# First normalization of a two-layer graph network moved into the second layer's block, with that layer's first builds

## What is computed

```python
def _L0_gnn_ref(node_feat, edge_feat, eps, src, dst):
    m = jax.nn.relu(node_feat[src] + edge_feat)
    neigh = jax.ops.segment_sum(m, dst, num_segments=node_feat.shape[0])
    return (1.0 + eps[0]) * node_feat + neigh

def _L1_gnn_ref(node_f, src, dst):
    n = node_f.shape[0]
    ones = jnp.ones(src.shape[0], dtype=node_f.dtype)
    out_deg = jnp.clip(jax.ops.segment_sum(ones, src, num_segments=n), 1.0)
    in_deg = jnp.clip(jax.ops.segment_sum(ones, dst, num_segments=n), 1.0)
    x = node_f * jax.lax.rsqrt(out_deg)[:, None]
    agg = jax.ops.segment_sum(x[src], dst, num_segments=n)
    return agg * jax.lax.rsqrt(in_deg)[:, None]

x = _layernorm(x + _L0_gnn_ref(x, edge_attr_32, L0_gnn_eps, src, dst), axis=-1)
x = _layernorm(x + _L1_gnn_ref(x, src, dst), axis=-1)
```

## Time and profile before

| | us |
|---|---|
| median of 3 runs | 5204.33 (5204.24 to 5209.14) |
| the profiled execution | 5206.82, its span 5205.0 |
| `layer_0`, first instruction to the last on DVE | 0 to 3949.0 |
| `finish_0`, first PE instruction to the last on DVE | 3951.0 to 3987.2 |
| `layer_1`, first on DVE to the last addition into `acc` | 3988.1 to 5167.6 |
| `finish_1`, from its first transpose | 5170.1 on |

### The profile page before, as it was taken

How to read it: one execution, slowest core, us unless ns; L and a number is a source line. 1 busy time by engine, 2 the same in 40 slices (tenths; PEclk the granted TensorE clock), 3 DMA queues, 4 the chain that set the end, 5 groups by cost and what they waited for, 6 DMA issues and landing times. The chain is left out here.

```text
span 5205.0 us, 62766 instructions
## 1 busy us (share of the span) xinstructions
PE 3317.5 (64%) x21148; PEld 1678.5 (32%) x21148; DVE 3284.0 (63%) x4730; ACT 2758.7 (53%) x2908; POOL 2961.1 (57%) x3134
## 2 busy tenths in 40 slices
PE   4555555555555555555555555555555999999997
PEld 1111111111111111111111111111113888888886
DVE  7766666666666666666666666666665444444445
ACT  4555555555555555555555555555554555555553
POOL 7777777777777777777777777777771000000000
PEclk7666666666666666666666666666666999999998
DMA  3333333333333333333333333333334999999995
GB/s 126 119 122 133 125 119 119 120 125 136 125 119 119 119 119 139 122 119 119 121 127 133 125 119 119 119 122 136 123 116 160 325 323 325 324 324 325 324 326 206
DMA packets 269134, 867.71 MB, mean 167 GB/s; under 512 B 90218, under 2 KB 140218, under 8 KB 252602
## 3 DMA queue, kind: packets, MB, share of 16 engines
q1 hardware_dynamic: 169107, 815.98, 42.2%
q0 software_dynamic: 100000, 51.40, 6.1%
HBM read 486.77 MB, written 380.38 MB: 167 GB/s over the span
## 5 line engine op out<-in xcount | busy, mean ns | idle before, releaser
L163 POOL DMA_INDIRECT rows<-in_x,src_t x3125 | 2959.4, 947 | 961.7 <-issue 947.2
L687 PE MATMUL built<-x_parts,b_hot 100*128 100x490 bf16 x3000 | 1291.6, 534 | 1757.0 <-ACT big L621 1742.7
L621 ACT ACTIVATE big<-built 128x980 bf16<-128x980 f32 x1500 | 1803.5, 1228 | 546.3 <-PE built L687 543.2
L687 PEld LDWEIGHTS built<-x_parts,b_hot 100*128 100x128 bf16 x3000 | 249.5, 111 | 2645.0 <-ACT big L621 2027.9
L870 PE MATMUL applied<-counts,x_parts 128*96 128x160 bf16 x12250 | 916.1, 233 | 1.4 <-ACT counts L828 1.4
L426 DVE TENSOR_TENSOR sum_ps<-sum_ps,rows 128x416 f32<-128x416 f32 x250 | 142.9, 572 | 1223.8 <-DMA rows<-in_x,src_t 1218.7
L667 PE MATMUL agg<-hot,msg 128*128 128x512 bf16 x3125 | 903.0, 440 | 4.9 <-DVE msg L456 4.9
L870 PEld LDWEIGHTS applied<-counts,x_parts 128*96 128x96 bf16 x12250 | 880.1, 123 | 64.9 <-ACT counts L828 2.3
L143 DVE TENSOR_TENSOR x_parts<-iota_ps,hk_g 100x3920 bf16<-100x3920 f16 x375 | 819.3, 2185 | 0.0
L828 ACT ACTIVATE counts<-built 128x980 bf16<-128x980 f32 x500 | 598.8, 1239 | 391.1 <-PE built L856 391.0
L143 DVE TENSOR_TENSOR hot<-iota_ps,s_hi 128x5252 bf16<-128x5252 f16 x250 | 691.4, 2766 | 0.0
(11 more groups left out here) (130 smaller groups left out, 1448.0 us busy)
## 6 DMA issues: line engine op xcount, KB each, us to landing
stash<-big SPq DMA_DIRECT2D x125, 2940.0 KB, 9.1
counts<-stash SPq DMA_DIRECT2D x250, 1470.0 KB, 8.7
rows<-in_x,src_t POOLq DMA_INDIRECT x3125
edge_t<-in_edge_attr SPq DMA_DIRECT2D x61, 800.0 KB
big<-in_dst SPq DMA_DIRECT2D x1, 1562.5 KB
big<-in_src SPq DMA_DIRECT2D x1, 1562.5 KB
src_t<-in_src SPq DMA_DIRECT2D x61, 24.8 KB
dst_t<-in_dst SPq DMA_DIRECT2D x61, 24.8 KB
```

Of the source, the lines that this page charges most:

```text
L163: gp.indirect_dma_start(rows_d[:, j, :], None, nodes, bass.IndirectOffsetOnAxis(ap=src_d[:, j:j + 1].bitcast(U32), axis=0),).then_inc(s, 16)
L621: sc.activation(stage[:, slot % 2, q, :, d0:d0 + 2 * SPAN].rearrange("p c (b d) -> p b c d", b=2), built[n % 2][:, :, 0:KEYS].rearrange("p ...
L687: last = te.matmul(built[n % 2][:, b, 0:KEYS], b_hot[:, r, t, :], key_hot[:, r, t, :], start=True, stop=True)
```

## The change

`finish_0` is taken out as a stage. Its four instruction lists become the functions `normalize_pe`, `normalize_dve`, `normalize_act` and `normalize_sp` inside `layer_1`, which are called ahead of `each` in the one block; `each` no longer calls step 0, whose work is spread over them. So:

- DVE does `chunk(0, 0)` ahead of the copy of `degree_t`, and `chunk(1, 1)` between `left(1, ...)` and `last_part(1, ...)`.
- PE does group 0's four builds one by one behind the transposes of packets 3, 4, 5 and 6, ACT their copies around `squares(0)`. The transposes use three PSUM banks instead of four (`sums[0]`, `sums[1]`, `small`), the degree's a half of `built[1]`.
- PE's step 1 waits for `f_table` 1 ahead of column 0 and for `f_table` 2 ahead of column 49, since no block's end stands between any more.
- `acc` gets 96 partitions: the first layer's sums stay on 0 to 32, the second's (`acc_1`) lie on 64 to 95, with `put` and the last transposes there too. The clearing of all of them is DVE's memset at the outset; ACT's clearing and `l_clear` are gone.
- `key_hot` moves to the third part of `big`, since the normalization uses the first two. The tile `zeros` is gone, and the tiles allocated behind it lie 32 bytes lower on each partition.

```diff
-        acc = sb("acc", [DE, P * C + W])
+        A1 = 64
+        acc_all = sb("acc", [A1 + D, P * C + W])
+        acc, acc_1 = acc_all[0:DE, :], acc_all[A1:A1 + D, :]
...
-        zeros = sb("zeros", [P, 1])
...
-                    V(ve.memset(acc[:, :], 0.0))
+                    V(ve.memset(acc_all[:, :], 0.0))
...
-                step(0, 0, 0)
+
                 step(1, 1, 0)
...
-                key_hot = big[0:TP, C * D:C * D + LT * KEYS].bitcast(BF16).rearrange("p (s t m) -> p s t m", s=2, t=LT)
+                key_hot = big[0:TP, 2 * C * D:2 * C * D + LT * KEYS].bitcast(BF16).rearrange("p (s t m) -> p s t m", s=2, t=LT)
...
-                agg = sums[0][0:D, 0:W]
+                agg = sums[0][A1:A1 + D, 0:W]
...
-                put = small[0:D, 2 * D:2 * D + W]
+                put = small[A1:A1 + D, 2 * D:2 * D + W]
...
+                turn = [sums[0], sums[1], small]
+                degree_ps = built[1][:, 1, :]
...
+                def build_first(te, n):
+                    if n >= 2:
+                        te.wait_ge(l_counts, n - 1)
+                    for b in range(2):
+                        t = 2 * n + b
+                        last = te.matmul(built[n % 2][:, b, 0:KEYS], hi_hot[:, 0, t, :], key_hot[:, 0, t, :], start=True, stop=True)
+                    last.then_inc(l_built, 1)
...
+                def normalize_pe(te):
+                    for q in range(4):
+                        last = te.transpose(degree_ps[0:YQ, q * X:(q + 1) * X], degree[:, q * YQ:(q + 1) * YQ], ident[0:X, 0:X])
+                    last.then_inc(f_count, 1)
+                    for k, (c0, n) in enumerate(FR):
+                        if k >= 3:
+                            te.wait_ge(f_used, k - 2)
+                        for t in range(n):
+                            last = te.transpose(turn[k % 3][:, t * DE:(t + 1) * DE], acc[:, c0 + t:c0 + t + (P - 1) * C + 1:C], ident[0:DE, 0:DE])
+                        last.then_inc(f_turn, 1)
+                        if 3 <= k < 3 + LP:
+
+                            if k == 3:
+                                te.wait_ge(l_chunk, 1)
+                                te.wait_ge(f_turned, 2)
+                            build_first(te, k - 3)
+
+                    te.wait_ge(f_used, len(FR))
...
+                    ve.memset(r_out[:, :], 1.0).then_inc(f_turned, 1)
+                    chunk(0, 0)
+                    ve.wait_ge(f_count, 1)
+                    ve.tensor_copy(degree_t[:, :, :], degree_ps[0:YQ, 0:4 * X].rearrange("p (q m) -> p q m", m=X)).then_inc(f_turned, 1)
...
+                    last_part(0, 2, 2)
+                    left(1, 3, 3)
+                    chunk(1, 1)
+                    last_part(1, 4, 4)
...
+                    copy_first(sc, 0)
+                    copy_first(sc, 1)
+                    squares(0)
+                    copy_first(sc, 2)
+                    copy_first(sc, 3)
+                    sc.wait_ge(f_degree, 1)
+                    sc.activation(r_out[:, :], r_out[:, :], ACT.Sqrt).then_inc(f_root, 1)
...
-                            if isinstance(k, int) and k == 0:
-                                chunk(0, 0)
...
-                                if isinstance(k, int) and k == 2:
-                                    ve.wait_ge(l_clear, 1)
                                 ve.wait_ge(l_moved, k - 1)
-                                window = acc[0:D, bass.ds(first, W)]
+                                window = acc_1[:, bass.ds(first, W)]
...
-                            if isinstance(k, int) and k == 0:
-                                sc.activation(acc[0:D, :], zeros[0:D, 0:1].to_broadcast([D, P * C + W]), ACT.Copy).then_inc(l_clear, 1)
...
+                                if isinstance(k, int) and k == 1 and c0 in (0, CC):
+
+                                    te.wait_ge(f_table, 1 + c0 // CC)
```

More of the change, by code:

```diff
@@ L188, in _ @@
                 V(ve.memset(ones[:, :], 1.0))
-                V(ve.memset(zeros[:, :], 0.0))
                 n = V(ve.memset(fold_r[:, :], 0.0))
@@ new lines, in normalize_sp @@
+                def normalize_sp(sp):
+                    sp.wait_ge(f_turned, 2)
+                    sp.dma_start(degree_d.rearrange("(q p l) -> p q l", q=4, l=L), degree_t[:, :, 1:X]).then_inc(f_degree_d, 16)
+                    sp.wait_ge(f_degree_d, 16)
+                    sp.dma_start(r_out[0:P - 1, :], degree_d[0:(P - 1) * C].rearrange("(p c) -> p c", c=C)).then_inc(f_degree_d, 16)
+                    sp.dma_start(r_out[P - 1:P, 0:TAIL], degree_d[(P - 1) * C:N].rearrange("(p c) -> p c", p=1)).then_inc(f_degree_d, 16)
+                    for k in range(2):
+                        for h in range(2):
+                            load_counts(sp, k, 0, h)
+                    for h, (c0, c1) in enumerate(PART):
+                        sp.wait_ge(f_table, h + 1)
+                        sp.dma_start(table.rearrange("(p c) d -> p (c d)", c=C)[:, c0 * D3:c1 * D3],
+                                     x_parts[:, c0:c1, :].rearrange("p c d -> p (c d)")).then_inc(s_out, 16)
@@ L815, in step @@
                                 ve.reciprocal(r_in[:, :], r_in[:, :]).then_inc(l_rin, 1)
+                        normalize_dve(ve, chunk)
                         each(ve, step, LAST)
@@ L903, in step @@
                             apply(CC + CC // 2, C)
+                        normalize_pe(te)
                         each(te, step, LAST)
@@ L913, in general_sums @@
             src_t, dst_t, rows, rel, dst_hot, agg = buffers
+            total = acc if layer == 0 else acc_1
             v0 = V.n
@@ L950, in _ @@
                     with when_lost(ve):
-                        ve.memset(acc[0:M, :], 0.0).then_inc(g_v, 1)
+                        ve.memset(total[0:M, :], 0.0).then_inc(g_v, 1)
                         with ve.Fori(0, groups) as g:
@@ L1287, in build @@
                 layer_0()
-                counts = later.enter_context(nc.sbuf_tensor("counts", [P, 2, HB + 1, C, CS], BF16))
-                finish_0()
+            counts = later.enter_context(nc.sbuf_tensor("counts", [P, 2, HB + 1, C, CS], BF16))
             layer_1()
```

265 lines of the change are left out of this document (115 added, 150 removed).

## The result

The changed kernel takes 5187.93 us in the median of 7 executions (5187.05 to 5192.55), the kernel before, run beside it on the same chip, 5204.33 (5203.87 to 5209.14, also 7). The ratio is 0.9969, with a 95% interval of 0.996 to 0.9978: 16.4 us less, where 15.7 was forecast. The forecast of 5188.6 us lies 0.7 us above the median.

What follows compares the result with a forecast made beforehand. POOL's gathers were taken to set the pace up to 3949 us and PE to bound 4100 to 5100. From the median 5204.33 us, -11.9 and -3.8 sum to -15.7, giving 5188.6 us; range 5185 to 5195.

Steps and rivals of the forecast that it cites:

- Layer 0 and the steady part: Layer 0's last gather stays where it was; additions into `acc` still follow each other every 9.24 us.
- the added 96-partition memset: DVE's clearing of `acc`, 63 partitions taller; its time does not go by partitions, so it costs nothing.
- The put's rival: All 125 steps: `put` writing partitions 64 to 95 costs PE time; +24.9 us net, median 5229; chance 0.05.
- The rival's price: Six `put` loads at 0.111 us instead of 0.057: 0.32 us a step, 40.6 us in all.
- The start of step 1: PE's first application at 3985.0 instead of 3996.93, with block end, chunk, builds and copies off the path: -11.9 us.
- The degree's way: Out-degree through memory, store to clamp, 12.4 us; copy starts 2.24 us later, so clamp moves to 3966.9.
- Builds and copies beside the normalization: Group 0's builds on PE between packets and copies on ACT cost nothing, with 1.3 us of cover or more.
- The root: ACT's root of 98 columns behind the copies and table load: at most 0.76 us, done by 3970.8.
- Step 1: PE's step 1 ends at 3998.7, taking 13.7 us instead of 17.5, with ACT's clearing gone: -3.8 us.
- the bounds, 12.0 and 18.3 us: Total gain if the clock stays down all through step 1 (12.0) or is up at 3989.45 already (18.3).
- the gain near 18: Total gain if the 24 applications ahead of the 1.2 us wait count toward the clock's rise; 15.7 otherwise.
- The rival of the clock that falls short: Clock rises only at the end of step 2; gain 4.4 us, median 5199.9, no measurable change; chance 0.07.

Runs made afterwards that it cites:

- the clearing alone: Kernel before with only the second layer's sums and put on partitions 64 to 95, cleared by the memset, no ACT clearing; 5197.88 us against 5205.27, ratio 0.9985.
- The kernel with the degree first: Changed kernel with DVE's `chunk(0, 0)` moved behind the copy of `degree_t` and the addition to `eps_t`; 5186.3 us, ratio 0.9964.
- the order's second run: Changed kernel, `chunk(0, 0)` behind the degree's copy, builds 2 and 3 behind the last transposes, their copies behind the root; third chip, 5835.45 us, ratio 0.9965.
- the order's first run: Changed kernel, `chunk(0, 0)` behind the degree's copy, builds 2 and 3 behind the last transposes, their copies behind the root; second chip, 5836.2 us.
- matmuls added: Changed kernel with 26 matmuls of unused result on PE ahead of step 1; second chip, 5837.35 us, 1.0 less than the changed kernel beside it.
- order, matmuls added: Changed kernel with `chunk(0, 0)` behind the degree's copy, builds 2 and 3 and their copies later, plus 26 unused matmuls ahead of step 1; 5834.12 us, ratio 0.9963.
- the first four experiments: First chip: kernel before with only partitions and clearing changed, 5197.88 us; changed kernel with ACT clearing, 5198.5, `chunk(0, 0)` behind the degree's copy, 5186.3, `zeros` back, 5190.02.

## Why the prediction was right

**Layer 0 and the steady part.** Both stayed as they were: the period is 9.235 us, and the added 96-partition memset is free, as argued. The put's rival got a chance of 0.05 and was refuted twice, by the changed kernel and by the clearing alone. Its six weight loads and matmuls in one step of the changed kernel (to be read against rows 8):

```profile
4016.23 0.34 PEld L1082 LDWEIGHTS small<-place_hot,slots 80*32 80x32 bf16 x6 [0.41 <-issue]
4016.24 0.51 PE L1082 MATMUL small<-place_hot,slots 80*32 80x128 bf16 x6
```

These are 0.34 and 0.51 us, to the hundredth what they were on partitions 0 to 31. The rival's price was wrong all the same. It set a sixth of the merged row, 0.057 us, against 0.111 us, the mean of single loads of 128 columns. A single one of the six loads lasts 0.097 us in the median of 750, before and after alike; against that, a load of 128 columns would cost some 0.014 us more, 10.5 us in all and not 40.6 (an estimate), which would not have turned the sign. Nor do these two rows bear out that a load's time follows its columns. The Trainium skill, "TensorE: Matmul & The Clock Gate", "LDWEIGHTS (loading the stationary operand)", gives a load's time by its number of columns alone, over 1.2 GHz. That the other place made no difference fits this; the size doesn't, since for 32 columns it comes to 0.027 us (an estimate by that page), and the traces show 0.097.

**The start of step 1: -11.9 forecast, -11.7 measured** from layer 0's end. The degree's way is the term that limits it: +2.24 us forecast, +2.26 measured at the clamp (the copy began 2.35 us later, and the way through memory was 0.08 shorter). From the clamp to the end of `last_part(0)` it is 18.04 us, before 18.03. What is missing is the hop to PE: 0.26 us (3986.65 to 3986.91), where the forecast had 0.1. What the end of the block is worth apart from the chunk, builds and copies behind it, no run measured; the timeline of before shows 0.91 us of idle for it on DVE.

**Builds and copies beside the normalization: nothing forecast, nothing seen on the path, though one term was too small.** For these times 1.68 us are taken off, by which all of it stood later from layer 0 on. A build between two packets costs PE 1.04 us, not 0.85: the packets at 3963.91 and 3966.64 stand 2.73 us apart, where one alone took 11.81 / 7 = 1.69. So packet 6 is ready 0.6 us later than forecast (3966.64 + 1.87 - 1.68 = 3966.8, not 3966.2), and ACT's last copy 0.4 later (3970.74 - 1.68 = 3969.1, not 3968.7). The root takes 0.29 us and not the 0.76 allowed for, and the cover is 1.5 us (3972.34 to 3973.82; 1.3 forecast). The kernel with the degree first shows how near the packets were to the path: with the clamp 2.1 us earlier, the last one becomes the wait.

**Step 1: -3.8 forecast, -4.46 measured.** The first build stood where it was forecast (3991.09 - 1.68 = 3989.41, against 3989.45), which makes the chunk's 3.0 us right. The wait ahead of it was 0.78 us instead of 1.2, because the 24 applications began 0.2 us later and took 3.40 us, not 3.2. The clock rose 4.2 us after the wait's end where 4.5 was taken, and most of the difference to 3998.7 (3999.98 - 1.68 = 3998.3) comes from that. Of the bounds, 12.0 and 18.3 us, the measured 16.16 lies between, nearer to the upper.

That the rise would be counted from the end of the wait gave the right time for this kernel, and doesn't hold for all. The stretches in which the clock rose in the kernel with the degree first and in the order's second run:

```profile
3984.00:3986.00 2.00, 1.22 (x8) 0.64 (x7) 2.00 (x2) 0.00 (x0) 0.00 (x0) 0.87 0.48 191
```

```profile
4630.00:4632.00 2.00, 1.64 (x16) 1.23 (x17) 1.97 (x4) 1.01 (x1) 0.00 (x0) 0.92 0.06 22
```

These put the rise at 3984.5 and 4630.3, 3.3 and 4.1 us after the first application: in the first the wait of 0.79 us for the chunk had not begun, in the second its 0.78 us were just ending. In the order's first run it came after 3.7 us. In the changed kernel, its two repetitions and the one with `zeros` back it came 8.4 to 8.8 us after the start, 4.2 to 4.6 us behind the wait. Of the Trainium skill's sentence in "TensorE: Matmul & The Clock Gate", Part 1 (The HAM clock gate), that "activity releases the throttle", the prediction said that it would let the 24 applications count and bring the gain near 18: in the three executions they did count (their step 1 is 2.0 us shorter), in the changed kernel not. The same section also speaks of "sustained matmul activity", which the prediction left out.

The prediction had nothing by which to tell the two cases apart, so that step 1 came out near its -3.8 is in part luck; with the early rise the gain would have been some 18.2 us (65.57 less 36.34 and 11.07), near the upper bound. What decides between them stays open. PE had been idle for 15.8 to 16.6 us before the three and for 17.5 to 17.8 us before the four, but the idle time alone doesn't order the rises: where PE then worked without a gap, it was idle for 1.4 us (before), 1.4 (clearing alone), 9.5 (matmuls added) and 7.7 (order, matmuls added), and the clock rose after 4.5, 4.3, 4.2 and 5.8 us. Where the start falls from one execution to the next is the other candidate; no run varied either alone.

**The rival of the clock that falls short** (0.07) didn't happen: the upper clock was reached within step 1 in every kernel.

## What to carry to other kernels

Where two stages meet, find the one instruction list that is the path through the seam (here DVE's) and count what each inserted piece does to it and to the transfer that it starts: the chunk's 3.0 us ahead of a store moved the clamp, and all behind it, by 2.3 us (DVE had waited 0.7 us at that place before, which the chunk fills). Put the next stage's preparation on engines that idle there, but look what would wait next: of the 2.2 us that the better place of the chunk promised, the builds' hold on the last transposes took 1.2. And a stall on PE costs more than its length where the clock falls in it and the work behind it starts slow again (5.15 us of stall cost 6.9 in the kernel before, 5.44 us cost 8.1 in the changed one with ACT's clearing).

## What was not expected of the hardware

The kernel before takes 5204 to 5205 us in the first comparison and beside the first four experiments, and 5855 on two other chips. In the profiles of the changed kernel, 645.4 us of the 645.8 between the first and the second chip are in layer 0; layer 1 has the same period to 0.01 us. ACT's waits between 1000 and 3900 us (engine, line, waited for: us in total, times, longest), first of the changed kernel on the first chip, then on the second (`remote` is a wait whose end no instruction or transfer in the trace explains):

```profile
ACT msg L607 <- DVE sum_ps L427: 601.4, 92, 7.4
ACT big L622 <- PE built L688: 402.9, 261, 3.5
```

```profile
ACT big L622 <- remote: 1123.4, 151, 15.3
```

On the second chip ACT stands 1,123 of 2,900 us before a copy into `big` whose wait ends by nothing that the trace names. In the program the one wait for a transfer ahead of that copy is for the stores to the `stash`, which must have read `big` before it is written again; so slower stores there are the likely cause, and it is only argued. POOL waits 408 us in the same unnamed way ahead of its gathers, while a gather itself takes the same time (a median of 945 ns on the first chip, 944 on the second). Whoever compares kernels of this kind has to do it on one chip; the difference made by the change was 16.4 us on the first, 17.1 and 18.4 on the others.

Two smaller ones. DVE's addition took 285 to 286 ns (medians of 125) with its tiles on partitions 64 to 95, in each kernel with the new place, and 276 on 0 to 31; it is hidden here. And the granted clock not only rose at different distances from the start of work, it also fell behind a wait of 2.33 us once (0.3 us after PE had gone on), and not behind one of 2.52 us in another kernel.
